# VectorE: x1's maximum moved behind the tile's maximum in rounds 14 to 23; GpSimd: the root moved behind rounding in rounds 24 to 27

## What is computed

```python
x = x + jnp.tanh(g_xattn[0]) * _L0_xattn_ref(_layernorm(x), ctx)   # fp8-like quantised product, 32 row tiles -> "x1"
x = x + jnp.tanh(g_ffn[0]) * _L0_ffn_ref(_layernorm(x), w0, gamma) # 8-bit activations: scale = max |.| over ALL rows of x1
x = x + jnp.tanh(g_xattn[1]) * _L1_xattn_ref(_layernorm(x), ctx, ctx)
x = x + jnp.tanh(g_ffn[1]) * _L1_ffn_ref(_layernorm(x), router_w, Wa, Wb)
```

## Time and profile before

| | |
|---|---|
| median of 3 runs | 1982.6 us (1981.23 to 1984.6) |
| profiled execution, its own time | 1981.46 us |
| its span, first to last instruction | 1979.7 us |
| mean granted TensorE clock | 0.988 |
| busy: PE, DVE, ACT, POOL | 1848.3, 1558.7, 1271.4, 846.7 us |
| first phase, to the last tile of x1 | about 460 us |

### The profile page before, as it was taken

How to read it: one execution, slowest core, us unless ns; L and a number is a source line. 1 busy time by engine, 2 the same in 40 slices (tenths; PEclk the granted TensorE clock), 3 DMA queues, 4 the chain that set the end, 5 groups by cost and what they waited for, 6 DMA issues and landing times.

```text
span 1979.7 us, 26468 instructions
## 1 busy us (share of the span) xinstructions
PE 1848.3 (93%) x8968; PEld 839.8 (42%) x8968; DVE 1558.7 (79%) x2378; ACT 1271.4 (64%) x2061; POOL 846.7 (43%) x1100
## 2 busy tenths in 40 slices
PE   1699999986699999999999999999999999999998
PEld 0344444432244444444444444444444444444443
DVE  8899999787877777777777777777777777777762
ACT  5698899665666665566666666665665666666650
POOL 3555565333444344344444444344344434443430
PEclk9999999998899999999999999999999999999999
DMA  9687866787888888888888888888888888888872
GB/s 213 170 206 199 229 200 179 187 206 223 160 149 165 175 169 172 170 166 157 169 170 164 174 163 169 168 173 171 168 163 163 169 163 172 169 167 170 151 151 60
DMA packets 923975, 340.50 MB, mean 172 GB/s; under 512 B 849728, under 2 KB 898880, under 8 KB 923840
## 3 DMA queue, kind: packets, MB, share of 16 engines
q1 hardware_dynamic: 923840, 338.81, 80.8%
HBM read 93.36 MB, written 33.55 MB: 64 GB/s over the span
## 4 chain that ended last, share of the span: by engine, by line
PE 73%; DVE 12%; issue 7%; SPq 3%; POOL 2%; DMA 2%; ACT 1%; POOLq 0%; DVEq 0%; ACTq 0%
PE sc L1106 16%; PE accs L1086 11%; PE accs L1087 11%; PE accs L1088 11%; PE accs L1127 6%; PE accs L1128 6%; PE accs L1129 6%; PE accs L1144 6%; SPq L336 2%; DVE tiny L1245 1%; DVE arena L1383 1%; DVE accs L1390 1%; DVE slot L1329 1%; DVE slot L1267 1%; DMA slot<-slot 1%
## 5 line engine op out<-in xcount | busy, mean ns | idle before, releaser
L1609 DVE SCALAR_TENSOR_TENSOR slot<-arena,tiny,slot 128x1024 f16<-128x1024 f32 x256 | 346.4, 1353 | 169.0 <-ACT slot L905 165.3
L905 ACT ACTIVATE slot<-arena,tiny 128x1024 f16<-128x1024 f32 x256 | 291.0, 1145 | 252.9 <-POOL tiny L717 247.0
L1106 PE MATMUL sc<-arena,slot 128*128 128x512 f16 x1536 | 375.9, 384 | 20.1 <-ACT arena L892 17.9
L715 POOL TENSOR_SCALAR tiny<-tiny 128x1 f32<-128x1 f32 x256 | 116.0, 453 | 519.6 <-ACT arena L892 519.6
L1604 DVE TENSOR_REDUCE tiny<-sc 128x1 f32<-128x1024 f32 x256 | 311.7, 1218 | 21.0 <-PE sc L1106 21.0
L892 ACT ACTIVATE arena<-sc,tiny,head_tab 128x1024 f32<-128x1024 f32 x256 | 308.4, 1205 | 8.6
L1106 PEld LDWEIGHTS sc<-arena,slot 128*128 128x128 f16 x1536 | 148.1, 98 | 212.1 <-ACT arena L892 31.5
L717 POOL TENSOR_TENSOR tiny<-tiny,neg_one 128x1 f32<-128x1 f32 x256 | 226.5, 885 | 21.3
L884 ACT ACTIVATE tiny<-tiny,head_tab 128x1 f32<-128x1 f32 x256 | 74.3, 290 | 206.5 <-DVE tiny L1604 206.5
L1127 PE MATMUL accs<-probs,arena 128*128 128x512 f16 x512 | 195.4, 382 | 9.9 <-issue 8.4
L1086 PE MATMUL accs<-wb_hi,slot 128*128 128x512 f16 x512 | 194.1, 379 | 2.7 <-DMA slot<-slot 2.7
(11 more groups left out here) (218 smaller groups left out, 2914.2 us busy)
## 6 DMA issues: line engine op xcount, KB each, us to landing
arena<-in_x SPq DMA_DIRECT2D x32, 512.0 KB, 4.1
x_scratch<-arena SPq DMA_DIRECT2D x32, 512.0 KB, 3.3
slot<-x_scratch SPq DMA_DIRECT2D x32, 512.0 KB, 3.2
slot<-in_ctx SPq DMA_DIRECT2D x32, 512.0 KB, 4.3
out<-arena SPq DMA_DIRECT2D x31, 512.0 KB, 3.6
slot<-in_L_ffn_Wa SPq DMA_DIRECT2D x12, 512.0 KB, 4.6
slot<-in_L_ffn_Wb SPq DMA_DIRECT2D x9, 512.0 KB, 5.3
wb_hi<-in_ctx SPq DMA_DIRECT2D x64, 64.0 KB, 2.4
```

The lines of the kernel that those rows point to most:

```text
L905: act.activation(high, full, ACT.Identity, scale=rinv[c % 4][:]).then_inc(s_ph.sem, 1)
L1106: mm = pe.matmul(sc[:, c % 2, h * HALF:(h + 1) * HALF], q[i][:, c * P:(c + 1) * P], k[j][:, h * HALF:(h + 1) * HALF], start=start, stop=stop)
L1609: dve.scalar_tensor_tensor(out=low, in0=full, scalar=rinv[c % 4][:], in1=high, op0=ALU.mult, op1=ALU.subtract).then_inc(s_pl.sem, 1)
```

## The change

On VectorE `x1_max(j-2)` stands behind `x_max(j+3)` in rounds 14 to 23; in all other rounds it stays ahead of `round_x` or of `finish_x1`. On GpSimd `x_rstd(j+4)` stands behind `x_round(j+2)` and `x_low(j+2)` in rounds 24 to 27 (there is no tile j+4 afterwards). No instruction is added or taken away.

```diff
@@ GpSimd @@
-                if is_x(j + 4) and j + 4 >= X_EARLY:
+                if j < PREP and j + 4 >= X_EARLY:
                     x_rstd(j + 4)
                 if is_x(j + 2) and j + 2 >= X_EARLY:
                     x_round(j + 2)
                     x_low(j + 2)
+                if j >= PREP and is_x(j + 4):
+                    x_rstd(j + 4)
@@ VectorE @@
                     x_stats(j + 4)
...
-                if is_x(j - 2):
+                if is_x(j - 2) and not SUM_FROM < j < PREP:
                     if j == 2:
                         dve.wait_ge(gsq.sem, 1)
                     x1_max(j - 2)
...
                     x_max(j + 3)
+                if SUM_FROM < j < PREP:
+                    x1_max(j - 2)
```

## The result

The changed kernel takes 1989.65 us (median of 12 runs, 1984.89 to 1992.25), the kernel before 1982.72 us over 12 runs beside it. The ratio is 1.0029, 95% interval 1.0020 to 1.0037, so 5.7 us (4.0 to 7.3) slower; the two medians by themselves are 6.9 us apart, inside the same interval. The forecast was 1988.4 us, 1985.6 to 1991.2, that is 5.8 us more than before.

The account below looks back on a forecast made before the run. ScalarE and VectorE set the first phase's round, TensorE close behind; the new two-engine lap becomes the bound. VectorE's part 5.8 us, GpSimd's part nothing: median 1982.6 + 5.8 = 1988.4 us, range 1985.6 to 1991.2.

Parts of the forecast that it names:

- The lap: Loop over ScalarE and VectorE, square to x_scale, mask, x1_max and back: 12.11 us a round against ScalarE's 11.77.
- Its start: Round 14: mask at 251.12 to 252.25, taken as 251.7, moving the square from 256.60 to 257.9.
- Its end: Square of round 21 at 342.7, transpose L1069 at 343.1, ScalarE's round 24 at 368.7: 5.6 us cost, 5.8 taken.
- Behind it: From round 28 on nothing differs; the end of the first phase keeps its distance from round 24.
- GpSimd's part: Rounds 24 to 27: x_round 2.2 us earlier, x_high unmoved, rounds still 13.0 us; booked at nothing.
- The first: Rival: square's hold isn't paid and the cover of L1301's padding pays, 1980.0 us; 4 in 100.
- The second: Rival: GpSimd's root is last after all, together with the hold, 1979.6 us; 4 in 100.
- third: Rival: GpSimd's root is last in rounds 24 to 27 and decides alone, 1973.8 us; 3 in 100.
- The fourth: Rival: lap longer than its pieces, GpSimd's 0.55 us root holding each of nine masks, 5.0 us more, 1993.4; 4 in 100.

Follow-up runs that it names:

- VectorE's part alone: Kernel before with only the VectorE hunk, x1_max behind x_max in rounds 14 to 23: ratio 1.0028 against the kernel before.
- the statistics early: Kernel before with x_stats(j+4) ahead of round_x(j+2) on VectorE in rounds 24 to 27: ratio 0.9977; with GpSimd's part as well, 0.9976.
- two buffers: Changed kernel with squares of odd tiles 13 to 23 in an unused SBUF tile, each waiting only for the maximum two tiles before: 0.9994 against the kernel before.
- GpSimd's part alone: Kernel before with only the GpSimd hunk, x_rstd later in rounds 24 to 27: ratio 1.0000 against the kernel before.
- one place earlier: Changed kernel with x1_max ahead of x_max instead of behind it: ratio 1.0004 against the kernel before.

## Why the prediction was right

- **The lap.** Forecast 12.11 us, measured 12.20. The pieces in the trace of after: square to mask 265.86 - 259.91 = 5.95 (forecast 3.46 + 2.46 = 5.92), mask to `finish_x1` 2.34, to `x_max` 1.40, to the maximum 1.14, the maximum 1.28 (all as in the earlier trace rows), and its release 272.11 - 272.02 = 0.09, where 0.03 was the shortest that the rows allowed. ScalarE's idle time was 0.31 us in full rounds (forecast 0.34), and that these agree so well is luck: from start to start a full round grew by 12.20 - 11.77 = 0.43 us, and the bracket counts only from the end of the instruction before, 0.1 us later than the start of the next where nothing waits.
- **Its start.** The mask of round 14 came in the free slot, 253.23 - 2.11 = 251.12, and then took 1.13 us: held by GpSimd's L611 (to 251.68 + 2.13 = 253.81), but not by the root, which came behind it at 253.76. The prediction took the rule of the Trainium skill (SBUF — State Buffer, "Who interferes with whom"), that whoever issues first keeps the port pair, to mean a wait for both GpSimd instructions and a start at 258.4. The mask was issued ahead of the root, so by the rule it waits for L611 alone; the trace agrees. The next square was at 259.91 - 2.11 = 257.80, forecast 257.9 between 257.3 and 258.4.
- **Its end.** The square of round 21 at 343.15 (forecast 342.7), the transpose at 343.46 (343.1), ScalarE's round 24 at 369.13 (368.7): + 6.04 us, where 5.6 were worked out from the rows and 5.8 taken. The missing 0.4 us are eight laps up to the square of round 22 that were 0.08 us longer each (0.06 of it the release), 0.7 us, less 0.1 us at the start and less 0.15 us from the mask of round 23 to ScalarE's round 24 (371.24 - 363.41 = 7.83, before 363.09 - 355.11 = 7.98).
- **Behind it** the forecast said that the distance is kept. It fell from 6.04 to 5.50 us at the end of the phase. The half microsecond came back where ScalarE waits for a weight's transfer, 4.48 us before and 3.98 us after. This wait lasts 3.91 to 4.52 us in the twelve traces, 4.28 in that of VectorE's part alone, whose 6.03 us at round 24 are still 5.91 at the end; so the forecast that the distance is kept holds to within what this wait varies.

```profile
443.24 1.15 ACT L811 ACTIVATE slot<-slot,tiny 128x1024 f32<-128x1024 f32 x1 [4.48 <-DMA slot<-in_L_ffn_Wa]
```

```profile
450.90 1.15 ACT L813 ACTIVATE slot<-slot,tiny 128x1024 f32<-128x1024 f32 x1 [3.98 <-DMA slot<-in_L_ffn_Wa]
```

- **GpSimd's part** was booked at nothing, and is nothing alone (1.0000), with the rest, and with the statistics early. The 12.99 us that were added up without it are what the early statistics shorten, 13.0 to 11.56 us.
- **The rivals.** The first, no hold and a cover that pays, fails twice: the hold is there, and with it gone (two buffers) no gain shows, - 0.08 us by the distance, though there the maximum of odd tiles is longer. The second and third, the root as the last wait, fall with GpSimd's part alone. The fourth, a lap longer than its pieces, is 0.09 us a lap and not 0.55; GpSimd held only the first mask.

## What to carry to other kernels

Before an instruction is moved to where its own engine has room, look up who waits for its result and what stands behind the waiter; if the mover in turn waits for something there, add up the whole lap and compare it with each engine's own round. Here a lap of 12.2 us, against 11.8 us of ScalarE in its full rounds and 10.4 to 10.7 in the shorter ones, cost 5.7 us in ten rounds, while one place earlier (11.04 us) no cost showed. The short rounds are easily overlooked: ten times the 0.43 us of a full round would be 4.3 us. A moved instruction that shortens a wait (GpSimd's root, 2.1 us earlier) is worth nothing unless its reader is free at that time; adding the pieces of a round up until they give its length shows which waits are in it, and which edit would pay.

## What was not expected of the hardware

A hold between VectorE and GpSimd works both ways and shows as a longer instruction, not as idle time. In the changed kernel the mask, issued 0.6 us before GpSimd's L611 ended, took 1.13 instead of 0.69 us, and GpSimd's root behind L611 took 1.09 instead of 0.55 us. With two buffers, where the maximum reads SBUF twice for odd tiles, it took 2.81 us instead of 1.22, and ended 1.08 us behind GpSimd's L602, and so (2.81 to 2.83 us) in each of rounds 15, 17, 19, 21 and 23; with one operand in PSUM it ran beside the same L602 of the next round in 1.22 us (VectorE, then GpSimd):

```profile
269.88 2.81 DVE L1395 CUSTOM_DVE_ANT_0 wb_lo<-wb_lo,slot 128x1024 f32<-128x1024 f32 x1
...
281.75 1.22 DVE L1395 CUSTOM_DVE_ANT_0 accs<-accs,slot 128x1024 f32<-128x1024 f32 x1
```

```profile
269.71 1.90 POOL L602 TENSOR_TENSOR slot<-slot 128x1024 f16<-128x1024 f16 x1
...
281.60 1.90 POOL L602 TENSOR_TENSOR slot<-slot 128x1024 f16<-128x1024 f16 x1
```

The Trainium skill (SBUF — State Buffer, "Who interferes with whom") says that a VectorE instruction with two SBUF inputs contends with a GpSimd instruction that reads SBUF, and one with at most one such input and outside the two-port modes doesn't. The trace agrees: 2.81 against 1.22 us. It also says that with a VectorE instruction in a two-port mode, which a `tensor_scalar` can be in, whoever issues first keeps the port pair for the whole instruction. The trace agrees with that order: the mask ended 0.55 us behind L611 (254.36 against 253.81), and the root, issued behind the mask, 0.49 us behind the mask (254.85).

A buffer in SBUF is thus no equal of one in PSUM for this instruction: 1.6 us longer in every second round. Most of it was hidden here, since VectorE had that time; in round 23 it also held GpSimd's L645, as told with that experiment.
